# Two graph layers on one core: type messages as extra rows of the slot sums, spread pad rows, early Q products, and identity products in TensorE's gaps

## The reference

```python
h = jnp.maximum(_layernorm(x), 0.0)                        # x: 3125 nodes x 256
# layer 0, 50000 edges sorted by dst
hp = relu(h @ W_pool.T + b_pool);  m = hp[src] * weight
neigh = segment_max(m, dst)                                # 0 where no edge
x = x + h @ W_self.T + b_self + (neigh @ W_neigh.T + b_neigh)
h = jnp.maximum(_layernorm(x), 0.0)
# layer 1
e = edge_emb[edge_type]                                    # 16 types
messages = ((h[src] + e) @ msg_W + msg_b) * gain + beta    # gain, beta from the task
edge_weight = 1 + edge_scale * tanh(gelu([h[src], h[dst], e, task] @ att_W1 + att_b1) @ att_W2 + att_b2)
agg = segment_sum(messages * edge_weight, dst) / max(segment_sum(edge_weight, dst), 1)
updated = gelu([h, agg * gain2 + beta2] @ up_W1 + up_b1) @ up_W2 + up_b2
x = x + layernorm(h + updated) * ln_g + ln_b
```

## Time and profile before

| | us |
|---|---|
| median of 3 runs | 1373.51 |
| lowest, highest | 1368.14, 1375.04 |
| the profiled execution, device time | 1371.06 |
| its span in the profile | 1369.3 |

### The profile page before, as it was taken

One profiled execution on the slowest core, in us unless ns is written; L12 is line 12 of the kernel. 1 busy time (PEld: TensorE's weight loads), 2 busy tenths in 40 slices (PEclk: granted clock), 3 DMA queues, 4 the chain that ended last, 5 costly groups with the idle time before them and its releaser, 6 DMA issues. The chain is left out here.

```text
span 1369.3 us, 18544 instructions
## 1 busy us (share of the span) xinstructions
PE 910.8 (67%) x4908; PEld 710.7 (52%) x4908; DVE 931.2 (68%) x2669; ACT 614.2 (45%) x1493; POOL 882.2 (64%) x892
## 2 busy tenths in 40 slices
PE   5602233332123511289997999999999999999795
PEld 4501122222112510167775777777777777777464
DVE  5366575665565644346747888888888888888347
ACT  5433332333233423222334665665665666565343
POOL 3377777777777777655065777777777777774012
PEclk9855555555555555589999999999999999999788
DMA  5378557566776565535665777777877777778302
GB/s 151 110 177 287 197 201 224 199 212 218 233 247 224 194 217 200 170 87 155 146 190 155 227 231 237 228 231 236 232 230 237 231 232 237 229 234 153 94 28 67
DMA packets 105123, 266.58 MB, mean 195 GB/s; under 512 B 25099, under 2 KB 45712, under 8 KB 98880
## 3 DMA queue, kind: packets, MB, share of 16 engines
q0 software_dynamic: 54560, 166.61, 42.5%
q1 hardware_dynamic: 48672, 97.03, 21.8%
q10 hardware_dynamic: 1792, 1.75, 0.5%
HBM read 195.82 MB, written 68.81 MB: 193 GB/s over the span
## 5 line engine op out<-in xcount | busy, mean ns | idle before, releaser
L681 POOL DMA_INDIRECT gath<-hp_d,chain_src x391 | 384.1, 982 | 131.8 <-issue 120.6
L1340 POOL DMA_INDIRECT gbuf<-pm_d,srcs x357 | 345.8, 968 | 124.3 <-issue 105.2
L918 DVE SCALAR_TENSOR_TENSOR hist<-hist,smask,gath 128x256 f32<-128x256 f32 x390 | 189.2, 485 | 205.3 <-ACT gath L714 197.1
L714 ACT ACTIVATE gath<-gath,chain_w 128x256 f32<-128x256 f32 x391 | 167.3, 496 | 334.0 <-DMA gath<-hp_d,chain_src 333.9
L1676 DVE TENSOR_TENSOR acc<-ps,acc 112x272 f32 x425 | 186.7, 439 | 70.0 <-DVE acc L1676 61.6
L1450 PE MATMUL ps<-qw,halves 128*128 x1275 | 209.6, 273 | 10.9 <-DVE halves L1661 8.1
L1452 PE MATMUL ps<-gbuf,ident 128*128 128x256 f32 x714 | 214.2, 382 | 0.0
L836 PE MATMUL ps<-win_hot,node_hot 128*112 128x28 bf16 x391 | 42.3, 247 | 230.9 <-DVE win_hot L1017 230.9
L1527 ACT ACTIVATE gbuf<-ps 128x512 f32<-128x512 f32 x180 | 107.4, 597 | 166.5 <-PE ps L1452 166.4
L1474 PE MATMUL ps<-gbuf,placed 128*112 128x272 f32 x714 | 178.9, 393 | 0.8 <-ACT placed L1548 0.4
L1450 PEld LDWEIGHTS ps<-qw,halves 128*128 128x128 bf16 x1275 | 125.0, 98 | 83.0 <-issue 14.4
(11 more groups left out here) (283 smaller groups left out, 1399.2 us busy)
## 6 DMA issues: line engine op xcount, KB each, us to landing
hist_d<-hist SPq DMA_DIRECT2D x48, 1024.0 KB, 4.5
gath<-hp_d,chain_src POOLq DMA_INDIRECT x391, 3.1
wn<-node_row_d SPq DMA_DIRECT2D x27, 224.0 KB
key<-node_row_d SPq DMA_DIRECT2D x26, 224.0 KB
gbuf<-pm_d,srcs POOLq DMA_INDIRECT x357, 3.9
pm_d<-gbuf SPq DMA_DIRECT2D x6, 896.0 KB, 5.0
hp_d<-hpo SPq DMA_DIRECT2D x7, 448.0 KB, 3.2
hb_d<-gbuf SPq DMA_DIRECT2D x7, 448.0 KB, 3.4
```

The source lines that it names most:

```text
L681: eng.indirect_dma_start(row_at(j), None, hp_d[:, :], bass.IndirectOffsetOnAxis(ap=chain_src[:, j:j + 1], axis=0)).then_inc(got[q % RINGG] ...
L714: eng.activation(row_at(j), row_at(j), ACT.Copy, scale=chain_w[:, j:j + 1]).then_inc(gw_ready, 1)
L918: eng.scalar_tensor_tensor(out=state_at(j), in0=state_at(j - 1) if j else first_state[:, :], scalar=smask[:, j:j + 1], in1=row_at(j), op0= ...
L1340: eng.indirect_dma_start(gath3(g % RING)[:, k, 0:2 * D], None, pm_d[:, :], bass.IndirectOffsetOnAxis(ap=srcs[:, g * SG + k:g * SG + k + 1] ...
```

## The change

**Block 1.** POOL's additions to x and their two loads go. DVE does stats one group earlier (`stats(i + 2)` behind `scales(i)` and ahead of the `hpb` add). The last group goes through DVE, ACT and SP in two halves. PE makes 26 products of the identity with itself after the weight transposes.

**Block 2.** The two biases become two rows in `own_rows` and enter the self product as a K = 2 product per window. The pad block's 32 sources become 0, 97, 194, ... in place of 0. PE makes 14 identity products once five states are left.

**Block 3.** 12 and 8 identity products follow choose(0) and choose(1). `keys_q` of groups 0 to 2 moves into the loop, behind `neigh`, with its steps on ACT and DVE. SP copies `em` into rows 112 to 127 of `acc`, once for each window.

**Block 4.** 8 identity products at the end.

**Block 5.** DVE multiplies the type columns by rd. `turn_types` turns the last 128 columns of each window by the identity, so that types land in rows 112 to 127; ACT copies rows 96 to 127 into `dg` and then writes the diagonals over rows 0 to 111. `update` is then four K = 128 products for each half, and the K = 16 products go. 14 and 6 identity products stand around the first two `turn_types`. `update(i)` waits for each half's bank alone, and rows_y(0) follows update(1).

```diff
@@ block 1, PE; DVE @@
+                for _ in range(26):
+                    eng.matmul(bank(6)[:, 0:P], ident[:, :], ident[:, :], start=True, stop=True)
...
                 stats(0)
+                stats(1)
                 for i in range(NG + 2):
-                    if i + 1 < NG:
-                        stats(i + 1)
                     if i < NG:
                         scales(i)
+                    if i + 2 < NG:
+                        stats(i + 2)
...
@@ block 1, POOL @@
-                for i in range(NG):
-                    eng.wait_ge(h_ready, i + 1)
-                    g3 = x3[:, i * GN:(i + 1) * GN, :]
-                    eng.tensor_tensor(g3, g3, bc(bself[:, :], GN), ALU.add)
@@ block 2 @@
+                        ins = eng.matmul(bank(6, 2)[0:WIN, k * D:(k + 1) * D], ones[0:2, 0:WIN], own_rows, start=False, stop=True)
...
+                eng.wait_ge(stepped, CH - 5)
+                for _ in range(14):
+                    eng.matmul(bank(2)[:, 0:P], ident[:, :], ident[:, :], start=True, stop=True)
                 eng.wait_ge(stepped, CH)
...
-                    eng.memset(padb[:, 0:BLK], 0.0)
+                    eng.tensor_scalar(padb[:, 0:BLK], iof[0:1, 0:BLK], 97.0, None, ALU.mult)
@@ block 3 @@
+                eng.dma_start(acc3[WIN:P, :, 0:D], bc(em[:, :], NT)).then_inc(em_in, 16)
...
                 def keys_q(i):
                     if i >= 2:
                         eng.wait_ge(q_res, i - 1)
+                    if i < QE:
+                        eng.wait_ge(n_put, i + 3)
+                        wait(eng, q_res, i)
...
                 choose(0)
+                keep_warm(12)
                 turn_n(0)
                 neigh(0)
                 choose(1)
+                keep_warm(8)
...
+                    if 1 <= i <= QE:
+                        keys_q(i - 1)
                     messages(i, range(3))
...
-                for i in range(NG):
+                for i in range(QE, NG):
                     keys_q(i)
@@ block 4, PE @@
+                eng.wait_ge(gelu_ready, (NGR - 1) * 2)
+                keep_warm(8, 2 * ((NGR - 2) % 2))
@@ block 5 @@
-                        at = (i * GN + k) * AW + D
-                        ins = eng.matmul(bank(i % 2)[0:TY, k * WIN:(k + 1) * WIN], acc[0:WIN, at:at + TY],
-                                         dg[i % 2][:, k * WIN:(k + 1) * WIN], start=True, stop=True)
+                        at = (i * GN + k) * AW + AW - P
+                        ins = eng.matmul(bank(i % 2)[:, k * WIN:(k + 1) * WIN], acc[0:WIN, at:at + P],
+                                         ident[0:WIN, 0:WIN], start=True, stop=True)
...
-                        eng.matmul(to[:, 0:GW4], em[:, f * P:(f + 1) * P], tt[i % 2][:, :], start=True, stop=False)
...
+                            ins = eng.matmul(to[:, k * WIN:(k + 1) * WIN], acc[:, at:at + P],
+                                             dg[i % 2][:, k * WIN:(k + 1) * WIN], start=True, stop=True)
...
+                keep_warm(14)
                 turn_types(0)
+                turn_types(1)
+                keep_warm(6)
                 for i in range(NG):
                     update(i)
-                    if i + 1 < NG:
+                    if 2 <= i + 1 < NG:
                         turn_types(i + 1)
-                    if i != 1:
-                        rows_y(max(i - 1, 0))
+                    if i >= 1:
+                        rows_y(i - 1)
...
+                eng.tensor_tensor(a4, a4, bi(rd[:, :], TY), ALU.mult).then_inc(scaled, 1)
```

More of the change, by code:

```diff
@@ L207, in x_parts, with halves_of @@
                 return 16 if i < NG - 1 else 48
+            def halves_of(o):
+                return [(0, GN)] if o < NG - 1 else [(0, GN // 2), (GN // 2, GN)]
             @block.sync
@@ L1236, in node_rows_of @@
                 return first_rows(i) if i < 2 else ngb[i % 2]
-            qf = qw[:, :].bitcast(fp32)
+            QE = 3
+            qf = qw[:, QE * GN * (3 * D):].bitcast(fp32)
             per = SG * RB * FLD * BLK
@@ L1247, in gnn_two_layers, with q_bank @@
             REC_AT, FLD_AT, COL_AT = 2, 4, NG - 1
+            def q_bank(i):
+                return bank(2, 2) if i < QE else bank(2 * (i % 2), 2)
             def rows_by_k(t):
@@ L1414, in turn_fields, with keep_warm @@
                         ins.then_inc(cols_ready, 1)
+                def keep_warm(n, b=6):
+                    for _ in range(n):
+                        eng.matmul(bank(b)[:, 0:P], ident[:, :], ident[:, :], start=True, stop=True)
                 choose(0)
+                keep_warm(12)
                 turn_n(0)
@@ L1506, in _ @@
                         put_n(i + 1)
+                    if 1 <= i <= QE:
+                        q_high(i - 1)
                     take(i, 0)
@@ L1510, in _ @@
                     take(i, 2)
+                    if 1 <= i <= QE:
+                        q_middle(i - 1)
                 eng.wait_ge(cols_ready, FLD)
                 eng.wait_ge(rows_out, 64)
-                for i in range(NG + 1):
+                for i in range(QE, NG + 1):
                     if i < NG:
-                        eng.wait_ge(q_ready, i + 1)
-                        eng.activation(qw3[0:WIN, i * GN:(i + 1) * GN, 0:D], rows_by_k(bank(2 * (i % 2), 2)[0:WIN, :]), ACT.Copy)\
-                           .then_inc(q_hi, 1)
-                    if i >= 1:
-                        eng.wait_ge(q_res, i)
-                        eng.activation(qw3[0:WIN, (i - 1) * GN:i * GN, D:2 * D], qr3, ACT.Copy).then_inc(q_mid, 1)
+                        q_high(i)
+                    if i > QE:
+                        q_middle(i - 1)
                 eng.wait_ge(one_set, 1)
@@ L1644, in _ @@
                     take(i, 3)
+                    if 1 <= i <= QE:
+                        q_lowest(i - 1)
                     if i == FLD_AT - 1:
                         slot_fields()
-                for i in range(NG):
-                    win = slice(i * GN, (i + 1) * GN)
-                    wait(eng, q_low, i)
-                    eng.wait_ge(q_hi, i + 1)
-                    eng.tensor_tensor(qr3, rows_by_k(bank(2 * (i % 2), 2)[0:WIN, :]), qw3[0:WIN, win, 0:D], ALU.subtract).then_inc(q_res, 1)
-                    eng.wait_ge(q_mid, i + 1)
-                    eng.tensor_tensor(qw3[0:WIN, win, 2 * D:3 * D], qr3, qw3[0:WIN, win, D:2 * D], ALU.subtract).then_inc(q_low, 1)
+                for i in range(QE, NG):
+                    q_residue(i)
+                    q_lowest(i)
                 eng.wait_ge(q_low, NG)
@@ L1708, in gnn_two_layers @@
             rd = s("rd", [WIN, NT], fp32)
-            dg = s2("dg", [WIN, GW4], fp32)
-            tt = s2("tt", [TY, GW4], fp32)
+            dg = s2("dg", [P, GW4], fp32)
+            HI = P - 32
             u = s2("u", [P, 2 * GW4], fp32)
@@ L1723, in gnn_two_layers @@
             dg_ready = sem("dg_ready")
+            scaled = sem("scaled")
             tt_ps = sem("tt_ps")
@@ L1775, in _, with keep_warm @@
             def _(eng):
+                def keep_warm(n):
+                    for _ in range(n):
+                        eng.matmul(bank(6)[:, 0:P], ident[:, :], ident[:, :], start=True, stop=True)
                 def turn_types(i):
-                    eng.wait_ge(dg_ready, i + 1)
+                    if i == 0:
+                        eng.wait_ge(scaled, 1)
                     if i >= 2:
```

90 lines of the change are left out of this document (52 added, 38 removed).

## The result

The changed kernel takes **1335.98 us** (median of four runs, 1334.87 to 1340.34), the kernel before beside it 1373.89 us. The ratio is 0.9754, with a 95% interval of 0.9724 to 0.9784: 2.5% faster. The prediction was 1341 us with a range of 1329 to 1356. The profiled execution took 1334.87 us (span 1333.1) in place of 1371.06 us (span 1369.3), so the forecast of -30.4 us has to be held against -36.2 us. The median lies at the lower edge of what the forecast called its own (1336 to 1345 us), between it and the fourth rival (1332 us).

What follows compares the result with a forecast made beforehand. POOL's gathers pace block 2, PE and POOL nearly equally block 4; clock-changing PE chains make blocks 1, 3 and 5. Terms -7.6 - 4.6 - 0.9 - 2.8 - 14.5 = -30.4 us from 1371.06 give 1341 us, range 1329 to 1356.

Steps and rivals of the forecast that it cites:

- fourth rival: PE's gap in block 5 too short for the clock to fall, transposes not held back: 1332 us, chance 0.10.
- Block 1: Early fast clock, DVE's new order and a halved last group end block 1 near 53.2 us: -7.6 us.
- Block 2: K = 2 products lie in PE's idle time while POOL sets the pace: 0 us.
- From block 2 to block 3: Identity products delay the closing transposes, but choose(0) and neigh(0) then run fast: -4.6 us, bounds -6.3 and +4.
- second price: Identity product on PE with overlapped ends: 0.25 us fast, 0.45 us slow; the forecast took 0.29 and 0.51.
- second rival: Identity products stand in the way between blocks 2 and 3: 1349 us, or 1353 with block 1 at -4; chance 0.14.
- Q products: Tail before block 4 shortens by 11.8 us, block 3's loop pays 10.9 us: -0.9 us, bounds -3 and +3.
- Pad rows: Spreading pad sources over 32 rows removes both PE waits late in block 4: -2.8 us, bounds 0 and -3.
- last eight products: PE's identity products at block 4's end finish 0.4 us after DVE's last sum: +0.4 us.
- Block 5: Earlier rows_y, one clock fall, then 6.9 us a group without K = 16 products: -14.5 us with block 4's end.
- first rival: The clock falls in steady block 5 as well, which then gives -8 us: 1347 us, chance 0.18.
- third rival: Block 4 turns from PE's pace to POOL's, slower than before: 1386 us, chance 0.03.

Runs made afterwards that it cites:

- no_identity2: Changed kernel without any of its 88 identity products, run again: 1341.7 us, beside the changed kernel at 1335.15 us.
- u1_first_warm4: Changed kernel with DVE's update(1) addition ahead of rows_y(0), and 28 identity products ahead of block 4: 1327.25 us, ratio 0.9662 to the kernel before.
- no_identity: Changed kernel without any of its 88 identity products, run when gathers landed late: ratio 0.987 to the kernel before.
- u1_first: Changed kernel with DVE's update(1) addition ahead of rows_y(0), run when gathers landed late: 1529.92 us, 0.986 of the kernel before.

## Why the prediction was right, and where it was off

**The number.** The terms missed by -7.8 us together, nearly all on one side, and the chain of block 2, for which nothing was forecast, came 2.0 us longer: -30.4 - 7.8 + 2.0 = -36.2 us. So the total lies nearer to the forecast than its terms do, by luck.

**Block 1, -7.6 forecast, -9.3 measured.** The step that failed is "POOL's seven additions were beside this path": they held DVE, for 3.4 us in the kernel before and 1.9 in the changed one. What the other edits give was judged about right or too high, by the kernels compared: 7.4 us with POOL's additions in both (60.8 to 53.4), 5.9 us with them in neither (57.4 to 51.5). The order and the halves give 4.3 us of it, the clock 1.2 to 1.6 us (0.4 on the old order). The first product ended at 21.0 us in place of 21.7, and the 4.65 us a group came out at 4.5 (bias additions from 21.15 to 43.52 us in five steps). The parts do not add exactly, because each moves what is waited for.

**Block 2, 0.** The chain came 2.0 us longer, within a scatter of 3 us among kernels that share its code, which the prediction did not allow for and which is as wide as several of its terms. That the K = 2 products cost nothing is not shown.

**From block 2 to block 3, -4.6 forecast, -6.1 measured.** The mechanism is right, and no_identity2 shows that it is the clock (5.4 of 6.1 us). The price of a product was mis-sized: 12 took 2.84 us, 0.24 each and not 0.29, and in u1_first_warm4 21 of their records, two to a product, start within 4.49 us at PEclk 0.50, 0.43 each and not 0.51. That is near the second price that the prediction named and did not take, 0.25 and 0.45 us. So the transposes started 5.1 us after the fifth last step and not 6, 2.5 us late and not 3.7, and turn_n(0) was not late at all. The second rival, identity products in the way, did happen in small form, in two of the kernels that share this code, for 1.4 to 1.6 us and not for 8.

**Q products, -0.9 and -1.5.** The tail gave 11.9 us (35.4 us before, 23.5 now; 11.8 forecast); the loop took 3.45 us more, three times (17.9 in place of 14.4 us), where 3.62 was forecast.

**Pad rows, -2.8, with +0.4 for the last eight products.** Block 4 became 2.0 and 1.6 us shorter; adding the pads alone won 2.4, and undoing them together with the Q products gave 3.8 us back, more than the bound of 3. That both waits go is as forecast.

**Block 5, -14.9 forecast, -19.3 measured.** The path was the one described, each step shorter. The first addition of rows_y was forecast 17.1 us into the block and came at 14.6: 20 identity products at 0.24 us, and everything fast behind them. The second came 13.5 us later, not 14.6: the clock did fall in the gap of 5.4 us (5.2 forecast), but it was high again by turn_types(3), 1.11 us where 1.9 was forecast. The steady pace was 6.7 us, not 6.9, and it is DVE's, whose 48.76 busy us are 7.0 for each of seven groups. The first rival, a clock that falls in the steady part, did not come: the clock stays up once PE is not made to stop. The new form is worth 15 us with identity products (88.2 against 73.2) and 16 to 17 without (92.5 against 75.7 to 76.9). How much of that is the K = 16 products and how much the new order of rows_y(0) behind update(1) was not taken apart. The rule of the Trainium skill ("TensorE: Matmul & The Clock Gate", LDWEIGHTS), by which the prediction had estimated 0.75 us more a group, does not fit this trace: eight loads of turn_types take 0.97 us with 128 columns and 0.69 us with 16, and PE's eight records 1.06 and 0.94 us, 0.1 us a group.

**The third rival**, block 4 at POOL's pace, was kept out by gathers that stayed as they were: busy and idle time less the 7.4 and 2.3 us that POOL waited for others, (343.8 + 114.7 - 7.4 - 2.3) / 357, is 1.26 us each, where the rival needed 1.29. At the time of the late gathers block 4 took 654 to 671 us, and no_identity and u1_first were only 1.3 and 1.4% faster than the kernel before, so block 4 can leave PE's pace. But that was not this rival: a gather kept POOL busy for 0.98 to 0.99 us, and POOL idled 67 to 77 us waiting for PE's sums.

**The fourth rival** came true in neither of its conditions: the clock did fall in block 5's gap (update(2) took 3.73 us), and the transposes were held back by 2.5 us. Its number was nearly met because each step was shorter than forecast.

## What to carry to other kernels

Filling PE's gaps with idle products paid where PE is waited for next (5.4 us between blocks 2 and 3) and hardly where it is not (0.4 us in block 1 of the old order), and even in the good place the clock can be low again two small gaps later. Before a queue is lengthened or filled, look whether an engine idles with its next-but-one input ready: one line moved on DVE gave 7.5 us of block 5, about as much as all 88 identity products (9.3 us by landmarks, 6.5 by the medians). An engine "beside the path" can still hold another, as POOL's additions held DVE's small instructions here.

## What the runs showed of the hardware that was not expected

- A POOL addition of 112x1024 (2.36 us) holds a DVE instruction of 112x4 with two SBUF inputs, or an addition of a constant in SBUF, until it ends: 0.17 became 1.68 and 1.84 us, 0.16 became 2.32 us. Reciprocal, statistics and PSUM reads were not held.
- An fp32 product of the identity with 128 columns costs 0.24 us at the high and 0.43 us at the low clock, a ratio of 1.8. Eight records of 256 columns (choose(0)) took 1.95 and 3.72 us, 1.9; sixteen of them (neigh(0)) 3.71 and 6.32 us, where the clock rose before the end.
- The chain of 391 gathers scatters by 3 us (509.2 to 512.4) between kernels that share its code, and the same chip had a time in which the kernel before took 1548 us in place of 1374. In the four kernels profiled at that time blocks 1 and 5 lasted as long as ever, and the chain and block 4, which gather, some 60 to 70 and 100 to 125 us longer.
